# Normalisations applied by ScalarE and GpSimd's products put ahead of its scatters in a decoder layer

## The reference

```python
def _layernorm(x, axis=-1, eps=1e-05):
    m = jnp.mean(x, axis=axis, keepdims=True)
    v = jnp.var(x, axis=axis, keepdims=True)
    return (x - m) / jnp.sqrt(v + eps)

# _L0_attn_ref: windows of 8 tokens, shifted by 4
qkv = xw @ w_qkv + b_qkv
attn = jnp.einsum('bhqd,bhkd->bhqk', q, k) * D ** (-0.5)
attn = jax.nn.softmax(attn + bias[None], axis=-1)
out = jnp.einsum('bhqk,bhkd->bhqd', attn, v)
# _L0_xattn_ref
q = x @ Wq
sim = jnp.einsum('bhid,bhjd->bhij', q, k) * SCALE
attn = jax.nn.softmax(sim, axis=-1)
out = jnp.einsum('bhij,bhjd->bhid', attn, v)
return out @ Wo + bo
# _L0_ffn_ref
logits = jnp.einsum('bsd,de->bse', x, router_w) + router_b
top1 = jnp.argmax(jax.nn.softmax(logits, axis=-1), axis=-1)
# for each expert i: a, g = split(x @ w1[i] + b1[i]); y = (a * sigmoid(g)) @ w2[i] + b2[i]
# the layer
x = x + _L0_attn_ref(_layernorm(x), ...)
x = x + _L0_xattn_ref(_layernorm(x), ctx_768, ...)
x = x + _L0_ffn_ref(_layernorm(x), ...)
```

## Time and profile before

| | us |
|---|---|
| median of 3 runs | 1498.8 (1496.0 to 1515.8) |
| profiled execution, time | 1501.7 |
| its span, first to last instruction | 1499.6 |
| TensorE busy | 1242.7 (83% of the span) |
| VectorE busy | 923.1 (62%) |
| GpSimd busy | 625.7 (42%) |
| ScalarE busy | 561.6 (37%) |

### The profile page before, as it was taken

How to read it: one execution, slowest core, us unless ns; L and a number is a source line. 1 busy time by engine, 2 the same in 40 slices (tenths; PEclk the granted TensorE clock), 3 DMA queues, 4 the chain that set the end, 5 groups by cost and what they waited for, 6 DMA issues and landing times. The chain is left out here.

```text
span 1499.6 us, 23663 instructions
## 1 busy us (share of the span) xinstructions
PE 1242.7 (83%) x8029; PEld 1015.5 (68%) x8029; DVE 923.1 (62%) x1531; ACT 561.6 (37%) x922; POOL 625.7 (42%) x474
## 2 busy tenths in 40 slices
PE   5998987775798658589777679998289999999996
PEld 3665665564566546456465467776289999999996
DVE  3786455458445565743565753443388888888784
ACT  1343322232222223231222233333166666666662
POOL 5444027427203735520654622211415555555652
PEclk9999998788899989699898889999599999999998
DMA  8324010010201001110010031110446676666660
GB/s 189 112 106 142 17 23 25 22 25 23 53 18 29 17 22 39 45 24 18 22 34 23 22 107 35 38 32 15 131 155 219 231 254 209 232 205 208 227 212 6
DMA packets 95338, 133.66 MB, mean 89 GB/s; under 512 B 42330, under 2 KB 76844, under 8 KB 89347
## 3 DMA queue, kind: packets, MB, share of 16 engines
q1 hardware_dynamic: 79299, 111.30, 23.6%
...
## 5 line engine op out<-in xcount | busy, mean ns | idle before, releaser
L1103 PE MATMUL psD<-vo,pT 128*128 128x128 f32 x1024 | 148.3, 297 | 87.5 <-DVE o L831 87.5
L1592 PE MATMUL psH<-xhigh,whigh 128*128 128x256 f32 x736 | 209.3, 284 | 8.0 <-DVE wlow L1440 6.5
L1592 PE MATMUL psH<-xlow,whigh 128*128 128x256 f32 x736 | 206.9, 281 | 0.0
L1592 PE MATMUL psH<-xhigh,wlow 128*128 128x256 f32 x736 | 206.8, 281 | 0.0
L1103 PEld LDWEIGHTS psD<-vo,pT 128*128 128x128 f32 x1024 | 138.5, 211 | 95.8 <-DVE o L831 91.2
L1440 DVE TENSOR_TENSOR wlow<-staged,whigh 128x2048 fp32r<-128x2048 f32 x69 | 158.3, 2295 | 0.0
L387 POOL TENSOR_TENSOR ve<-mv,eps 128x2 f32<-128x2 f32 (+1 forms) x36 | 7.1, 197 | 361.4 <-DVE mv L762 221.8
L1592 PEld LDWEIGHTS psH<-xhigh,whigh 128*128 128x128 f32 x736 | 141.1, 192 | 8.8 <-issue 6.8
L1509 ACT ACTIVATE whigh<-staged 128x2048 fp32r<-128x2048 f32 x69 | 132.3, 1918 | 28.1 <-PEq L146 15.1
L1015 PE MATMUL psA<-xT,wq 128*128 128x256 f32 x512 | 131.3, 408 | 12.6 <-ACT xT L561 12.6
L1592 PEld LDWEIGHTS psH<-xlow,whigh 128*128 128x128 f32 x736 | 140.0, 190 | 0.0
...
## 6 DMA issues: line engine op xcount, KB each, us to landing
...
```

What stands on the lines that cost most here:

```text
L1103: ins = mm(ps[:, m * P:(m + 1) * P], pT[:, (2 * w + m % 2) % 4, (m // 2) * N + t * P:(m // 2) * N + (t + 1) * P], vo[:, 4 * w + m, :], sta ...
L1592: ins = mm(psH[:, q % 2 * PAIR + c, part, :], lhs, rhs, start=i == 0, stop=i == len(passes) - 1)
```

## The change

- GpSimd makes, beside the scale `rs2`, a shift `nb2` = -mean * scale (`scale_and_shift`, four small operations in place of two). ScalarE applies norm2 and norm3 as `Identity(scale * x + bias)` with both as per-partition operands, two activations of 128x256 each; VectorE's `tensor_scalar` pairs go. In ScalarE's queue norm2 stands ahead of `round_keys`, norm3 behind `queries_kept(1)`.
- TensorE's transposes of norm2's rows stand between the two halves of X2 instead of behind them. The fourth `output_turn` moves behind the loop over head outputs.
- GpSimd: in a turn the next group's products stand ahead of `bias_x1`, `add_projection_bias` and norm2, the scatter of a sequence's row numbers moves into the next sequence (except for b = 3), product 1 moves from b = 1 to b = 0, product 7 and value product 3 stand ahead of the scatter, value product 2 ahead of norm3 of b = 2.
- VectorE: the sums that stood together ahead of PV0 are spread between head outputs, and two value sums move from b = 3 into b = 2. The exponential of the softmax moves from behind S3 to behind S5.
- `rowi` has two buffers, and the semaphore `scattered` one for each parity.

```diff
+            def scale_and_shift(i, ready, signal, value):
+
+                pool.wait_ge(ready, value)
+                s.done(nc.gpsimd.tensor_tensor(ve2[:, i], mv2[:, i, :, 1], eps[:, 0:2], ALU.add))
+                s.done(nc.gpsimd.tensor_tensor(rs2[:, i], ve2[:, i], half_exp[:, 0:2], ALU.pow))
+                s.done(nc.gpsimd.tensor_tensor(nb2[:, i], mv2[:, i, :, 0], rs2[:, i], ALU.mult))
+                then(pool, nc.gpsimd.tensor_tensor(nb2[:, i], zeros[:], nb2[:, i], ALU.subtract), signal, value)
+
             def norm2(j):
-                rstd(mv2[:, 0, :, 1], ve2[:, 0], rs2[:, 0], 2, var2, rstd2, j + 1)
+                scale_and_shift(0, var2, rstd2, j + 1)
 
             def norm3(j):
-                rstd(mv2[:, 1, :, 1], ve2[:, 1], rs2[:, 1], 2, var3, rstd3, j + 1)
+                scale_and_shift(1, var3, rstd3, j + 1)
...
+            def scatter_ids(j, b):
+
+                pool.wait_ge(routed, j + 1)
+                then(pool, nc.gpsimd.tensor_copy(id_now[:, b, :],
+                                                 id_all[:, bass.ds(j, 1), :].rearrange("p a k -> p (a k)")),
+                     id_ready, j + 1)
+                nc.gpsimd.tensor_tensor(idle2[:], eps[:, 0:1], eps[:, 0:1], ALU.add)
+                for half in range(2):
+                    nc.gpsimd.indirect_dma_start(
+                        out=ids[:, :], out_offset=bass.IndirectOffsetOnAxis(ap=rowi[:, b % 2, half:half + 1], axis=0),
+                        in_=id_now[:, b, half:half + 1], in_offset=None).then_inc(scattered[b % 2], 16)
+
             def turn(g, more):
                 n = g + 1
                 for b in range(GB):
                     j = g * GB + b
                     last = not more and b == GB - 1
-                    bias_x1(j, b)
-                    if not last:
-
-                        add_projection_bias(j + 1, b + 1, (g * 2 + (b + 1) // 2 + 1) * 32)
                     if more and b == 0:
                         rstd1_of(n)
                     if more and b == 1:
-                        for i in range(1, 6):
+                        scatter_ids(j - 1, b - 1)
+                        for i in range(2, 6):
                             product_of(n, i, i, False)
                     if more and b == 2:
-                        for i in range(7, WS):
-                            product_of(n, i, i, False)
+                        product_of(n, 7, 7, False)
+                        scatter_ids(j - 1, b - 1)
                         pool.wait_ge(probs_ready, n + 1)
                         for i in range(2):
                             product_of(n, WS + i, i, True)
                     if more and b == 3:
-                        for i in range(2, WS):
+                        product_of(n, WS + 3, 3, True)
+                        scatter_ids(j - 1, b - 1)
+                        for i in range(4, WS):
                             product_of(n, WS + i, i, True)
+                    if not more and b > 0:
+                        scatter_ids(j - 1, b - 1)
+                    bias_x1(j, b)
                     if not last:
+
+                        add_projection_bias(j + 1, b + 1, (g * 2 + (b + 1) // 2 + 1) * 32)
                         norm2(j + 1)
-                    norm3(j)
                     if more and b == 0:
                         pool.wait_ge(wd_done, 1 + WD_ITEMS * (n + 1))
-                        product_of(n, 0, 0, False)
+                        for i in range(2):
+                            product_of(n, i, i, False)
                     if more and b == 1:
                         product_of(n, 6, 6, False)
+                    if more and b == 2:
+                        product_of(n, WS + 2, 2, True)
+                    norm3(j)
 
                     pool.wait_ge(normed3, j + 1)
                     nc.gpsimd.tensor_tensor(idle2[:], eps[:, 0:1], eps[:, 0:1], ALU.add)
                     for half in range(2):
                         nc.gpsimd.dma_start(half_of(tokens_of, j, half), out_rows[:, b % 2, half, :])\
                             .then_inc(tokens_stored[b % 2], 16)
-                    pool.wait_ge(routed, j + 1)
-                    then(pool, nc.gpsimd.tensor_copy(id_now[:, b, :],
-                                                     id_all[:, bass.ds(j, 1), :].rearrange("p a k -> p (a k)")),
-                         id_ready, j + 1)
-                    nc.gpsimd.tensor_tensor(idle2[:], eps[:, 0:1], eps[:, 0:1], ALU.add)
-                    for half in range(2):
-                        nc.gpsimd.indirect_dma_start(
-                            out=ids[:, :], out_offset=bass.IndirectOffsetOnAxis(ap=rowi[:, half:half + 1], axis=0),
-                            in_=id_now[:, b, half:half + 1], in_offset=None).then_inc(scattered, 16)
+                    if b == GB - 1:
+                        scatter_ids(j, b)
...
+            def normalise(dst, src, i, ready, signal, value):
+
+                act.wait_ge(ready, value)
+                for half in range(2):
+                    ins = nc.scalar.activation(dst[:, half, :], src[:, half, :], ACT.Identity,
+                                               bias=nb2[:, i, half:half + 1], scale=rs2[:, i, half:half + 1])
+                then(act, ins, signal, value)
+
+            def norm2(j, b):
+                normalise(xn, x1[:, b % 2], 0, rstd2, normed2, j + 1)
+
+            def norm3(j, b):
+                normalise(out_rows[:, b % 2, :, 0:C], out_rows[:, b % 2, :, C:2 * C], 1, rstd3, normed3, j + 1)
...
-                        if more and b == 2 and u == 3:
-                            act.wait_ge(shifted, n + 1)
-                            then(act, nc.scalar.activation(probs[:], probs[:], ACT.Exp), exped, n + 1)
                         if more and b == 0 and u in (3, 5):
                             window_turned(n, u - 3)
                             window_turned(n, u - 2)
+                        if more and b == 2 and u == 5:
+                            act.wait_ge(shifted, n + 1)
+                            then(act, nc.scalar.activation(probs[:], probs[:], ACT.Exp), exped, n + 1)
...
+                        norm2(j + 1, b + 1)
                         round_keys(j + 1)
                         normed_turned("XN2'", xT, j, b)
                         queries_kept(0, j, b)
                         queries_kept(1, j, b)
+                    norm3(j, b)
                     normed_turned("XN3", xT3, j, b, last)
...
-                    if more and b == 2:
-                        sum_scores(n, 5)
-                    if more and b == 3:
-                        sum_values(n, 0)
-                        sum_values(n, 1)
                     if more and b == 0:
                         norm1_stats(n)
                     if more and b == 1:
@@ -815,11 +843,8 @@
                         sum_scores(n, 1)
                     if more and b == 2:
                         sum_scores(n, 6)
-                        sum_scores(n, 7)
-                        window_shift(n)
                     if more and b == 3:
                         sum_values(n, 2)
-                        sum_values(n, 3)
                     for u in range(CH):
                         ps, value = full(f"PV{u}", j, b)
 
@@ -836,22 +861,25 @@
                         if more and b == 0 and u >= 2:
                             for part in QKV_PARTS[u]:
                                 window_qkv(n, *part)
-                        if more and b == 1 and u in (1, 3, 5):
+                        if more and b == 1 and u % 2:
                             sum_scores(n, 2 + u // 2)
-                        if more and b == 2 and u == 2:
+                        if more and b == 2 and u == 0:
+                            sum_scores(n, 7)
+                            window_shift(n)
+                        if more and b == 2 and u == 3:
                             window_divide(n)
-                        if more and b == 3 and u in (1, 3, 4, 6):
-                            sum_values(n, {1: 4, 3: 5, 4: 6, 6: 7}[u])
+                        if more and b == 2 and u >= 6:
+                            sum_values(n, u - 6)
+                        if more and b == 3 and u in (1, 2, 4, 5, 7):
+                            sum_values(n, {1: 3, 2: 4, 4: 5, 5: 6, 7: 7}[u])
 
                     last = not more and b == GB - 1
                     if not last:
                         start_sequence(j, b)
-                        norm2(j + 1, b + 1)
...
-                    dve.wait_ge(rstd3, j + 1)
-                    for half in range(2):
-                        ins = nc.vector.tensor_scalar(xn3[:, half, :], mine[:, half, :], mv2[:, 1, half, 0:1],
-                                                      rs2[:, 1, half:half + 1], ALU.subtract, ALU.mult)
-                    then(dve, ins, normed3, j + 1)
                     if not last:
                         maxima(0, j, b)
                         maxima(1, j, b)
```

(9 more changed lines are left out.)

28 lines of the change are left out of this document (13 added, 15 removed).

## The result

| | before | after |
|---|---|---|
| median of the runs, us | 1500.6 (1496.0 to 1515.8) | 1525.3 (1516.0 to 1530.6) |
| ratio to before, 95% interval | 1 | 1.0143 (1.0099 to 1.0186) |
| profiled execution: time, span, us | 1501.7, 1499.6 | 1523.2, 1521.5 |
| mean granted clock of TensorE | 0.92 | 0.91 |

The changed kernel is 1.4% slower. The prediction was 1485 with a range of 1458 to 1520: a gain was forecast and a loss came, 5 us above the upper end. (The ratio is the one on record; the two medians alone would give 1.6%.)

What follows compares the result with a forecast made beforehand. TensorE was taken to bound heads without window work, VectorE's and GpSimd's order those with it. Three groups at -7.2 gave -21.6; with +6.3, +0.7 and +0.7 outside, -13.9 in total: 1485 us, 8 in 10 within 1458 to 1520.

Steps and rivals of the forecast that it cites:

- The step that failed: Tail, TensorE behind norm3's transposes: later work keeps its waits, so each tail GpSimd did not disturb grows by 2.1 us.
- Rival (2): Tails: the new wait drops TensorE's clock; with nine of sixteen tails affected, +46 us, 1531; chance 0.14.
- The pair on ScalarE: Norm2 and norm3 on ScalarE: two 128x256 activations taken at 0.9 us, bounds 0.6 and 1.1.
- The head of b = 1: From the cast to `rowi` to the query matmuls, b = 1: 34.5 us against 38.62, so -4.1.
- The wait inside X2: TensorE between X2's halves, waiting for ScalarE's norm2: 0.9 us, about 4 in b = 1; 0.8 added for the clock.
- The head of b = 2: From the cast to `rowi` to the query matmuls, b = 2: 41.4 us against 40.35, so +1.1.
- The head of b = 3: From the cast to `rowi` to the query matmuls, b = 3: 42.2 us against 53.03, so -10.8.
- PV0 from 4.35: Start of the head of b = 2: first head output taken from 4.35 to 5.0 us after the cast to `rowi`.
- The tails of b = 1, 2 and 3: From query matmuls to the next `rowi` cast: +1.1, +3.4 and +2.1 us, including `cand` held by products, 2.1 and 1.3.
- The tail of b = 0: From query matmuls to the next `rowi` cast, b = 0: two products now ahead of norm3, no change.
- Rival (3): Head of b = 3: sums and products still alternate and the 10.8 us is lost; 1517 us; chance 0.13.
- Rival (1): Cheap ends: small operations not held, no clock loss in X2, short b = 2 and 3 ends, pair 0.6; 1459 us; chance 0.18.

Runs made afterwards that it cites:

- version 4: Changed kernel with five idle matmuls of 128x256 ahead of the XN3 transposes in the last turn, filling the wait for norm3: 1512.9 us, ratio 1.004 to before.
- experiment 2: Kernel before with norm3 alone moved to ScalarE, nothing else of the change: 1522.8 us, ratio 1.012 to before.
- experiment 6: Changed kernel with both norms back on VectorE and norm2's transposes behind X2, leaving only the reordering of GpSimd and the sums: 1466.1 us, ratio 0.976 to before.
- Experiment 8: Order-only kernel (1466 us) with the scatter of row numbers put ahead of product 7 and value product 3 again: 1477.4 us, ratio 0.980 to before.
- The ladder: Four kernels, one step each: order only with bias additions ahead of norm1's scale 1460.8 us, order only 1466.1, norm3 alone back on VectorE 1472.4, changed kernel 1525.3.
- experiment 5: Changed kernel with norm2's transposes back behind both halves of X2, both norms still on ScalarE: 1510.3 us, ratio 1.004 to before.
- 10: Order-only kernel with bias additions ahead (1460.8 us), value products 2 and 3 and value sums 0 and 1 moved back into b = 3: 1463.7 us, ratio 0.974 to before.

## Why the prediction was wrong

Forecast and measurement lie 35.8 us of the span apart (-13.9 and +21.9): 19.8 of them in the last turn, 13.0 in the window turns, 6.3 in the start-up, and -3.3 in the expert stage. In the window turns the heads of b = 2 and 3 miss by 21.2 and the tails came out 7.9 better than forecast. Two terms of about the same size failed, then: the price of the new wait in the last turn, which comes first here, and the start of the heads of b = 2 and 3.

**The step that failed** is this one of the tail: "Behind them on TensorE stand queries 2, the logits, queries 3, the ranks and the next sequence's scores, each with the same waits as before: the tail grows by 2.1". The wait was right: forecast Q + 5.9, measured Q + 5.98. The matmuls behind it were priced as at full clock. That holds in version 4, where the wait is filled (tail 15.51; 15.4 was forecast), and not in the kernel after (19.4). The last turn, forecast at +7.0, came at +26.8, and 17.1 of that went when five idle matmuls a sequence kept TensorE busy (178.8 to 161.8). That filling the wait gives the time back is shown; why the clock fell in these tails and kept up in those of experiment 2, behind the same 2.09, is not. Rival (2) named this mechanism, gave it 0.14 and asked nine of sixteen tails for it. Its price was wrong in form. The tails with window work mostly kept their clock (16.1 to 16.9 us at b = 1 and 2), three tails of the last turn lost 3.9 us each, and two of the heads behind them, which the rival had left out, lost 2.5 each. Of the 28.0 that the window turns lost when norm3 went to ScalarE, 19.3 are in tails, nearly all of it the wait itself; the other 9, in heads, are no more than executions of the same code differ by.

The argument against the rival was the error of judgement. "With a wait of 3 us the tail of b = 1 kept 1.00 in the row shown" is one row out of the two in the earlier trace rows; the other had 0.64, and it was the very stretch that cost 5.1 us. The last turn was never asked at all, though it was the one place where every us of TensorE's is a us of the span: the earlier trace rows shows it busy for 25.04 of 25.92.

**The pair on ScalarE** was taken as 0.9, within 0.6 and 1.1, and measured 1.09. The estimate of 1.08 from the figures of the Trainium skill (ScalarE: Activation LUTs, What ACT_TABLE_LOAD costs) agrees with this trace. It would have been the better term, and its 6 us would not have changed the sign.

**The head of b = 1**: 34.5 forecast, 33.6, 35.2 and 35.2 measured. The wait inside X2 and a falling clock behind it were both in the sum: Q comes 10.3 after the addition in two of the three and 8.6 in the third. The wait itself, forecast at about 4, was 1.4 and twice 3.1 (in b = 2, 2.7 to 2.8).

**The head of b = 2**: 41.4 forecast; 43.5, 45.5 and 43.7 measured. The head of b = 3: 42.2 forecast; 46.1, 46.3 and 46.4 measured. Here the mechanism was right (in b = 3 the first division no longer waits behind products, and each product was ready before its sum) and the sizes were off. The term is the start, "PV0 from 4.35", which the earlier trace rows shows at full clock. In the timeline of the kernel after, the first rows of b = 2 and of b = 3, with T0 at 531.74 and 593.28:

```profile
532.81 1.14 PE L1101 MATMUL psA<-qT,kT 64*77 64x256 f32 x4
534.45 1.14 PE L1101 MATMUL psA<-qT,kT 64*77 64x256 f32 x4
538.55 0.18 DVE L855 RECIPROCAL rden<-psD 128x4 f32<-128x4 f32 x1 [4.23 <-PE psD L1126]
599.95 0.18 DVE L855 RECIPROCAL rden<-psD 128x4 f32<-128x4 f32 x1 [2.73 <-PE psD L1126]
```

The score matmuls of b = 2 take 1.14 instead of 0.66, so the first head output comes at T0 + 6.8, and in b = 3 at T0 + 6.7, some 2.4 later than taken. In b = 3 VectorE stands idle for 2.73 before it, with the next sum behind the division in its order. The three heads of b = 3 make 12.9 of the miss, those of b = 2 8.3 (the change of each against the change that was forecast). The late start, some 2.3 us in each, is about two thirds of it; the rest is open. Norm3 on ScalarE is not the reason: with the order alone (experiment 6) these heads are 44.1, 44.1 and 41.2, and 45.7, 45.8 and 44.1. The prediction's own sign, a head of b = 3 above 46, came up, by 0.1 to 0.4. Its terms for this head (4.0, eight of 0.65, five of 3.7) also add up to 27.7 and not to 28.5, a slip in the other direction. Clocks again: before, the heads of b = 3 ran at 0.74 and I had assumed a full clock in their first 5 us.

**The tails of b = 1, 2 and 3** with window work: 17.5, 16.6 and 15.3 forecast; 16.8 to 16.9, 16.1, and 15.6 with one of 17.0 measured. The order in which they stand is explained by the held `cand`, forecast at 2.1 and 1.3 from products of 4.54 and 3.68. The timeline of the kernel after, b = 1 and b = 2:

```profile
275.17 4.53 POOL L288 TENSOR_TENSOR tmp<-staged 128x2048 f32<-128x2048 f32 x1
277.66 2.08 DVE L905 TENSOR_TENSOR cand<-lg,best 128x16 f32<-128x16 f32 x1
335.61 3.69 POOL L288 TENSOR_TENSOR tmp<-staged,probs 128x2048 f32<-128x2048 f32 x1
338.12 1.22 DVE L905 TENSOR_TENSOR cand<-lg,best 128x16 f32<-128x16 f32 x1
```

An operation on 16 columns that takes 0.17 alone takes 2.08 and 1.22, and ends as the product ends (279.70 and 279.74; 339.30 and 339.34). This is the rule of the Trainium skill (SBUF — State Buffer, Who interferes with whom) that was read as applying to small operations too; this trace agrees. Experiment 8 does not price the hold: in its base, the order alone, the rows are stored earlier, the product in the tail of b = 1 runs from Q + 4.6 to 9.1, and no `cand` is held (all sixteen take 0.17 to 0.18).

**The tail of b = 0**: no change forecast, 18.0, 18.2 and 16.5 against 18.3 and 18.1. Right, with XN3 at Q + 7.11 where 6.9 was forecast. "No 4.9 us normalisation anywhere" was wrong: the ones of norm2 and norm3 are gone, and norm1's of 4.94 appeared.

**The start-up**: +7.0 where +0.7 was forecast. "The further edits cost nothing: they lengthen no queue named above" was said without looking at the start-up's own order. The ladder splits the 7.0 (and the 1.3 that the reordering had gained): 3.6 for the bias additions beside norm1, 3.3 for norm2, 1.4 for norm3.

**The expert stage** was 3.3 us shorter, with no part of the change in it; no run was made for that.

**Rival (3)** is out: in b = 3 each product stood ready, and these heads fell by 6.5 us in the mean. **Rival (1)** asked four things to go well, and none did throughout: `cand` was held, Q came 10.3 behind the addition in several heads, the ends of b = 2 and 3 came late, and the pair took 1.09. But with norm3 on VectorE and the bias additions ahead the kernel comes to 1460.8, where (1) had put the changed one.

**What stays open**: whether two waits (0.90 inside X2, 2.09 in the tail) cost more than the sum of both, and what brings the lower level in this tail. 2.09 did in the kernel after and in experiment 5; 1.34, made on VectorE, did not; but neither did 2.09 and 2.37 in the tails of experiment 2, made by ScalarE. So it is not the length of this one wait alone, and no version had the same length by both engines. Single heads of 27.4 instead of 25.9 us appear also in versions without any added wait (6, 8, 10), and nothing tried here says why there.
